# Layer 2: the normalisation of a pair's rows moves from VectorE to ScalarE, ahead of the second gate

## The chip, the cores and the metric

One core of a Trainium2 chip runs the whole program. The metric is device time in microseconds (us). Five engines work beside each other, each through its own queue in program order: PE (TensorE), DVE (VectorE), ACT (ScalarE), POOL (GpSimd) and SP, which only starts transfers here. They meet through semaphores.

## What is computed

Two layers over x of 2 x 1024 tokens by 256. Each layer normalises the tokens, runs an attention and a feed-forward block on them, and adds attention times silu(feed-forward) to x. The change is in layer 2, whose attention runs between the two batch rows of a token (so it is small), and whose feed-forward is two linear layers, each with a layer norm ahead of it:

```python
x = x + s * g                       # end of layer 1
xn = _layernorm(x, axis=-1)
s = _L1_attn_ref(xn, L1_attn_weight_qkv, L1_attn_weight_proj)
g = _silu(_L1_ffn_ref(xn, L1_ffn_w_fc, L1_ffn_w_proj))
x = x + s * g
# in _L1_ffn_ref: bitlinear(x, w) = layer_norm(x) @ ternarized(w).T (with a fine quantisation)
h = bitlinear(x, w_fc)
h = jax.nn.gelu(h, approximate=False)
return bitlinear(h, w_proj)
```

## The kernel before, in words

The 2048 tokens are 16 tiles of 128 (one token to a partition, 256 values in a row). Layer 1 (attention with 16 query heads, and 64 experts with gathered tokens) fills the first 300 us. Layer 2 takes the tiles in eight pairs: pair p holds tiles p and p + 8, which are the two rows of the batch for the same 128 positions.

The order of layer 2 is written out by hand, once for each engine, as a loop over p from -3 (`AHEAD` = 3) to 7. Turn p of every loop works on several pairs at once: it ends pair p, runs the hidden layer of pair p + 1, takes the moments of pair p + 2, and gates layer 1's output of pair p + 3. There is no scheduler; a queue does what its loop says, in that order.

- VectorE, turn p: `low_x(p+1)` (L1213, the low half of the turned x), `sum_squares(p)` (L1250), `moments(p+2)` (L1182 to L1191: statistics of the pair's rows, the last two steps each 128 x 2 numbers from `mv1` into `nv`), `spreads(p)` (L1256 to L1259: the variance for pair p's second norm, with L1258 squaring 128 x 2 numbers of `st3`), `low(p+1,0)` (L1243), `newton(p)` (L1150 to L1152, after GpSimd's root), `half_scale(p)` (L1267, `zhalf`), `normalise(p+2)` (L1203: rows minus mean, times 1/std, into `xh`; then two small steps for `kvscale`), `products(p+1)`, `low(p+1,1)`, `score_difference(p+1)`, `silu2(p)` (L1275), `silu(p+3)` (L1172), `low(p+1,2)`, `attended(p)` (L1284) and `low(p+1,3)`. Each `low` needs ScalarE's `square` of the same quarter.
- ScalarE, turn p: `high_x(p+1)`, `half_tanh(p)`, two quarters of the hidden layer (`hidden(p+1,0)`, `hidden(p+1,1)`, each gelu L770, copy L777, square L783), `take_attT(p)`, `gate(p+3)`, `take_kv(p+1)` (L762, L763), `gate2(p)` (L808, which waits for `zhalf`), then quarters 2 and 3.
- GpSimd, turn p: `weigh(p)` (L524), `total(p+3)` (L505, L506), `gated(p+3)` (L512), `roots(p)` (L537: the power -0.5 of all variances), `add_gated(p+3)` (L517, after VectorE's `silu`), `finish(p)` (L531, after VectorE's `attended`). Turn 5 and later have no `total` and no `gated`, since there is no pair p + 3.
- TensorE, turn p: `turn_x(p+1)` (transposes of `xh`), `down1(p, 0..3)` (L1647, after `silu2(p-1)`; quarter 3 needs `low(p,3)`), `fc(p+1, 0..1)`, `turn_att(p)`, `square_sums(p)` (L1654), `qkv(p+1)`, `fc(p+1, 2..3)`, `project(p)`.

TensorE's part of a turn comes about half a turn behind VectorE's. A "loop" below is the time from one start of `roots` (L537) to the next.

Of the kernel before, what the change touches and what calls it, by code (L numbers as in the profile page):

```python
# [9 lines left out]
ACT = mybir.ActivationFunctionType  # L10
ALU = mybir.AluOpType
AX = mybir.AxisListType

P = 128
# [50 lines left out]
NP = NT // 2  # L65
GT = 2
# [22 lines left out]
def build(nc, q, router, Wkv, Wo, shared, sd, wgu_d, wdn_d, wqkv, wpo, wpo4, wfc, wpj, out):  # L89
# [9 lines left out]
    with ExitStack() as ctx:  # L99
        def sb(name, shape, dt=F32):  # L100
            return ctx.enter_context(nc.sbuf_tensor(name, shape, dt))

        def sem(name):
            return ctx.enter_context(nc.semaphore(name))
# [3 lines left out]
        def bk_(i):  # L108
            return two[i // 2][:, (i % 2) * 512:(i % 2) * 512 + 512]


        x = sb("x", [P, NT, D])
# [98 lines left out]
        def l1(n):  # L211
            at[0] += n
            assert at[0] <= 10752, at
            return F[:, at[0] - n:at[0]]

        xh = [l1(GT * D).rearrange("p (q d) -> p q d", q=GT) for _ in range(2)]
# [32 lines left out]
        mv1 = sb("mv1", [P, GT, 2])  # L249
        st3 = sb("st3", [P, 2, GT])  # L250
        msq, ratio = sb("msq", [P, GT]), sb("ratio", [P, GT])
        kvscale, zhalf = [[sb(f"{n}{i}", [P, GT]) for i in range(2)] for n in ("kvscale", "zhalf")]
        gwc = sb("gwc", [P, 1])
        nv, ny, nt2 = [sb(n, [P, 3 * GT]) for n in ("nv", "ny", "nt2")]
        expo = sb("expo", [P, 3 * GT])
        warm = sb("warm", [P, 1])
# [36 lines left out]
        acc_ready, gated_ready, gate_ready, silu_ready, x1_ready, xh_ready, xT1_ps, xT_hi_ready, xT_lo_ready = [  # L293
            sem(n) for n in ("acc_ready", "gated_ready", "gate_ready", "silu_ready", "x1_ready", "xh_ready", "xT1_ps",
                             "xT_hi_ready", "xT_lo_ready")]
# [3 lines left out]
        cs_ps, wpj2_ready, wpo_ready, fc_ps, gelu_ready, sq_ready, sqsum_ready, zhalf_ready, hi_ready, lo_ready = [  # L299
            sem(n) for n in ("cs_ps", "wpj2_ready", "wpo_ready", "fc_ps", "gelu_ready", "sq_ready", "sqsum_ready",  # L300
                             "zhalf_ready", "hi_ready", "lo_ready")]
        v_in, root_ready = sem("v_in"), sem("root_ready")
        z_ps, ztanh_ready, zu_ready, out_ready, out_last, out_stored = [sem(n) for n in (
            "z_ps", "ztanh_ready", "zu_ready", "out_ready", "out_last", "out_stored")]

# [34 lines left out]
        def root_cols(p):  # L340

            return slice(0 if p + 2 < NP else 2 * GT, 3 * GT if p >= 0 else 2 * GT)
# [69 lines left out]
        def _(pool):  # L412
# [120 lines left out]
            def roots(p):  # L533

                c = root_cols(p)
                pool.wait_ge(v_in, p + 3)
                pool.tensor_tensor(ny[:, c], nv[:, c], expo[:, c], ALU.pow).then_inc(root_ready, 1)  # L537

            for p in range(-AHEAD, NP):
                if p >= 0:  # L540
                    weigh(p)
                if 0 < p + AHEAD < NP:
                    total(p + AHEAD)
                    gated(p + AHEAD)
                if p >= -2:
                    roots(p)
                if 0 < p + AHEAD < NP:
                    add_gated(p + AHEAD)
                if 0 <= p < LAST:
                    finish(p)  # L550

        @block.scalar
        def _(sc):
# [181 lines left out]
            def gate(p):  # L735
                if p:
                    sc.wait_ge(acc_ready, p)
                else:
                    sc.wait_ge(tot_first, 1)
                if p == 2:  # L740
                    sc.wait_ge(x1_first, 1)
                elif p > 2:
                    sc.wait_ge(x1_ready, p - 2)
                for q_ in range(GT):
                    t = p + NP * q_
                    sc.activation(tg[p % 2][:, q_, :], tot[:, t, :], ACT.Tanh, scale=half_rden[:, t:t + 1]).then_inc(gate_ready, 1)

            def high_x(p):
                sc.wait_ge(xT1_ps, p + 1)
                if p:  # L750
                    sc.wait_ge(fc_ps, FC * p)
                    sc.wait_ge(qkv_ps, p)
                sc.activation(xT_hi, bk_(0).rearrange("p (k n) -> p k n", k=KH), ACT.Copy).then_inc(xT_hi_ready, 1)

            def take_kv(p):

                sc.wait_ge(scale_ready, p + 1)
                sc.wait_ge(qkv_ps, p + 1)
                if p >= 2:
                    sc.wait_ge(attT_ps, p - 1)  # L760
                old = bk_(1)[:, QKV1:512].rearrange("p (g c) -> p g c", g=NKV1)
                sc.activation(kv0[p % 2], old, ACT.Copy, scale=kvscale[p % 2][:, 0:1])  # L762
                sc.activation(own[p % 2][:, 0], old[:, :, HD1:2 * HD1], ACT.Copy, scale=kvscale[p % 2][:, 0:1])\  # L763
                    .then_inc(kv_ready1, 1)
# [21 lines left out]
            def hidden(p, j):  # L786

                if p < NP:
                    gelu(p, j)
                    high(p, j)  # L790
                    square(p, j)

            def half_tanh(p):
                sc.wait_ge(dif_ready, p + 1)
                if p:
                    sc.wait_ge(tdv_ready, p)
                sc.activation(td[:, :], dif[:, :], ACT.Tanh, scale=kvscale[p % 2][:, 1:2]).then_inc(td_ready, 1)

            def take_attT(p):
                sc.wait_ge(attT_ps, p + 1)  # L800
                sc.activation(attT, bk_(6)[:, 0:3 * P].rearrange("p (k n) -> p k n", k=3), ACT.Copy).then_inc(attT_ready, 1)

            def gate2(p):
                sc.wait_ge(zhalf_ready, p + 1)
                if p:
                    sc.wait_ge(zu_ready, GT * p)
                for q_ in range(GT):
                    sc.activation(tz[:, q_, :], z_bank(q_)[:, 0:D], ACT.Tanh, scale=zhalf[p % 2][:, q_:q_ + 1])\  # L808
                        .then_inc(ztanh_ready, 1)

            for p in range(-AHEAD, NP):
                if 0 <= p + 1 < NP:
                    high_x(p + 1)
                if p >= 0:
                    half_tanh(p)
                if p + 1 >= 0:
                    hidden(p + 1, 0)
                    hidden(p + 1, 1)
                if p >= 0:
                    take_attT(p)  # L820
                if p + AHEAD < NP:
                    gate(p + AHEAD)
                if 0 <= p + 1 < NP:
                    take_kv(p + 1)
                if p >= 0:
                    gate2(p)
                if p + 1 >= 0:
                    hidden(p + 1, 2)
                    hidden(p + 1, 3)

        @block.vector
        def _(ve):
# [7 lines left out]
            def then(ins):  # L840
                ve.wait_ge(dve, mark(ins))
# [261 lines left out]
            for n in range(NE):  # L1103
                ve.wait_ge(gtanh_ready, n + 1)
                if n >= 2:
                    ve.wait_ge(hT_ps, n - 1)
                then(ve.scalar_tensor_tensor(out=h[n % 2], in0=eth[n % 2], scalar=1.0, in1=gu[n % 2][:, 0:FF],  # L1107
                                             op0=ALU.add, op1=ALU.mult))
# [89 lines left out]
            def normalise(p):  # L1198

                if p >= 2:  # L1200
                    ve.wait_ge(xT1_ps, p - 1)
                for q_ in range(GT):
                    ve.tensor_scalar(xh[p % 2][:, q_, :], x[:, p + NP * q_, :], mv1[:, q_, 0:1], ny[:, GT + q_:GT + q_ + 1],  # L1203
                                     ALU.subtract, ALU.mult).then_inc(xh_ready, 1)
                then(ve.tensor_tensor(ratio[:, :], nv[:, GT:2 * GT], ny[:, GT:2 * GT], ALU.mult))
                if p >= 2:
                    ve.wait_ge(kv_ready1, p - 1)
                ve.scalar_tensor_tensor(out=kvscale[p % 2][:, :], in0=ny[:, 0:GT], scalar=1.0 / WSCALE, in1=ratio[:, :],
                                        op0=ALU.mult, op1=ALU.mult).then_inc(scale_ready, 1)
# [88 lines left out]
            for p in range(-AHEAD, NP):  # L1298
# [14 lines left out]
                if 0 <= p + 2 < NP:  # L1313
                    normalise(p + 2)
# [413 lines left out]
```

## Time and profile before

| what | value |
|---|---|
| time, median of 3 runs (lowest, highest) | 428.29 us (426.84, 429.66) |
| the profiled execution's own time | 431.49 us |
| its span, first to last instruction | 429.8 us |
| busy: PE, PEld | 342.5 us (80%), 268.9 us (63%) |
| busy: DVE | 301.1 us (70%) |
| busy: ACT | 209.4 us (49%) |
| busy: POOL | 252.3 us (59%) |

The shares are means over the whole span; layer 2 is its last quarter, and each engine's share there is another. Busy is what an engine spent in instructions, and an instruction that is held up inside counts as busy for all of that time. In a timeline the start of an instruction may lie a tenth before the end of the one ahead of it on its engine, because they overlap; the step from start to start is then what one of them costs its engine.

### The profile page before, as it was taken

What the parts mean: (1) busy time and instruction counts of PE and PEld (TensorE: products, weight loads), DVE (VectorE), ACT (ScalarE), POOL (GpSimd) and SP (SyncE); (2) the same over time, 40 slices, a digit from 0 to 9 for tenths busy, and PEclk for the clock granted to TensorE, in tenths of its full rate; (3) what the DMA queues carried; (4) which work ended last, traced back from release to release, by engine and by line L of the source; (5) the groups of instructions that cost most, each with busy time, mean ns of one, the idle gap of its engine ahead of it and who ended that gap; (6) DMA issues with size and microseconds to landing.
All of it is one profiled execution on the core that took longest, in us unless ns stands there. A gap on an engine that the chain in (4) does not pass through costs nothing.

```text
span 429.8 us, 7084 instructions
## 1 busy us (share of the span) xinstructions
PE 342.5 (80%) x2108; PEld 268.9 (63%) x2108; DVE 301.1 (70%) x950; ACT 209.4 (49%) x536; POOL 252.3 (59%) x237
## 2 busy tenths in 40 slices
PE   0997688997989898989889888694078878987893
PEld 0983345675767677767676676483056766776773
DVE  4699744647858765546575656844668998899875
ACT  3734235444623463564343344321147678676871
POOL 3682034756867766678887888754456545764211
PEclk9999599998989999999999999979569999999999
DMA  8855933557775879878778786534920000000001
GB/s 281 350 179 152 361 97 95 108 119 174 158 184 115 230 173 278 247 174 198 144 177 187 148 193 138 90 38 56 317 69 0 26 2 25 26 25 27 2 24 51
DMA packets 33033, 58.42 MB, mean 136 GB/s; under 512 B 3723, under 2 KB 20451, under 8 KB 32611
## 3 DMA queue, kind: packets, MB, share of 16 engines
q1 hardware_dynamic: 20707, 39.08, 27.8%
q0 software_dynamic: 12288, 18.88, 24.6%
q8 instruction: 18, 0.29, 0.3%
q14 instruction: 20, 0.16, 0.1%
HBM read 40.22 MB, written 17.73 MB: 135 GB/s over the span
## 4 chain that ended last, share of the span: by engine, by line
PE 35%; DVE 26%; issue 11%; DMA 10%; ACT 9%; POOL 6%; DVEq 0%; POOLq 0%; SPq 0%; ACTq 0%
PE two L1523 5%; PE two L1503 5%; DMA W<-tok_d,idxE 4%; DMA acc_d<-W,idxE 4%; PE two L1463 4%; PE two L1535 4%; DVE F L1250 3%; PE two L1388 2%; POOL ny L537 2%; PE two L1512 2%; ACT W L783 2%; POOL W L478 2%; ACT two L770 2%; POOL acc_d L497 2%; PE two L1414 2%
## 5 line engine op out<-in xcount | busy, mean ns | idle before, releaser
L497 POOL DMA_INDIRECT acc_d<-W,idxE x64 | 103.3, 1614 | 48.9 <-DVE W L1071 30.6
L478 POOL DMA_INDIRECT W<-tok_d,idxE x56 | 57.4, 1025 | 41.6 <-DVE idxE L1033 24.8
L1107 DVE SCALAR_TENSOR_TENSOR W<-W,two 128x88 f32<-128x88 f32 x64 | 15.5, 242 | 57.8 <-ACT W L702 45.1
L686 ACT ACTIVATE W<-two 128x256 f32<-128x256 f32 x64 | 24.4, 380 | 43.6 <-PE two L1512 39.0
L1503 PE MATMUL two<-A,v 128*128 128x128 f32 x256 | 34.9, 295 | 6.7 <-issue 5.9
L1503 PEld LDWEIGHTS two<-A,v 128*128 128x128 f32 x256 | 33.7, 208 | 9.5 <-issue 8.9
L1647 PE MATMUL two<-W,A 128*128 128x257 f16 x256 | 30.1, 273 | 11.3 <-DVE F L1275 10.0
L1614 PE MATMUL two<-F,wfcT 128*128 128x256 f16 x256 | 32.8, 280 | 4.3 <-DVE A L1243 2.9
L1647 PEld LDWEIGHTS two<-W,A 128*128 128x128 f16 x256 | 23.9, 98 | 17.2 <-DVE F L1275 11.8
L770 ACT ACTIVATE two<-two,gwv 128x512 f32<-128x512 f32 x32 | 21.3, 665 | 23.3 <-PE two L1614 23.3
L1463 PE MATMUL two<-kT,vT 128*128 128x512 f32 x64 | 30.4, 597 | 2.6 <-DVE F L1024 1.4
L1523 PE MATMUL two<-W 128*128 128x176 f32 x160 | 31.9, 324 | 0.0
L1512 PE MATMUL two<-ident,W 128*128 128x128 f32 x112 | 22.7, 286 | 11.0 <-DMA W<-tok_d,idxE 9.9
L1071 DVE TENSOR_SCALAR W<-two,W 128x256 f32<-128x256 f32 x56 | 26.8, 478 | 5.8 <-PE two L1535 2.8
L1614 PEld LDWEIGHTS two<-F,wfcT 128*128 128x128 f16 x256 | 24.9, 100 | 9.4 <-issue 4.2
L1512 PEld LDWEIGHTS two<-ident,W 128*128 128x128 f32 x112 | 14.5, 146 | 24.1 <-DMA W<-tok_d,idxE 14.2
L952 DVE TENSOR_REDUCE nmax<-two 128x1 f32<-128x1024 f32 x16 | 19.6, 1223 | 11.8 <-PE two L1463 9.9
L517 POOL TENSOR_TENSOR x<-x,F 128x512 f32<-128x512 f32 x7 | 8.9, 1272 | 31.3 <-DVE F L1172 31.3
L1523 PEld LDWEIGHTS two<-W 128*128 128x128 f32 x160 | 25.1, 198 | 0.6 <-issue 0.4
L1535 PE MATMUL two<-W 88*128 88x256 f32 x80 | 24.3, 385 | 1.1 <-DVE W L1071 0.7
L1243 DVE TENSOR_TENSOR A<-two,A 128x512 f16<-128x512 f32 x32 | 21.9, 683 | 2.5 <-ACT W L783 2.0
L663 ACT ACTIVATE A<-two,nmax 128x1024 f32<-128x1024 f32 x16 | 17.8, 1114 | 11.7 <-DVE nmax L952 10.3
(239 smaller groups left out, 877.6 us busy)
## 6 DMA issues: line engine op xcount, KB each, us to landing
W<-in_gu SPq DMA_DIRECT2D x20, 352.0 KB
acc_d<-F SPq DMA_DIRECT2D x2, 2176.0 KB, 14.5
F<-in_gu SPq DMA_DIRECT2D x12, 352.0 KB
W<-in_dn SPq DMA_DIRECT2D x20, 176.0 KB
tok_d<-xr SPq DMA_DIRECT2D x2, 1280.0 KB, 5.8
F<-in_dn SPq DMA_DIRECT2D x12, 176.0 KB
x<-in_q SPq DMA_DIRECT2D x4, 512.0 KB, 6.6
A<-in_Wo SPq DMA_DIRECT2D x1, 2048.0 KB, 12.9
```

Of the source, the lines that this page charges most:

```text
L478: pool.indirect_dma_start(out=xg[n % XR], out_offset=None, in_=tok_d[:, :], in_offset=bass.IndirectOffsetOnAxis(ap=idxE[:, n:n + 1], axis=0))\
L497: pool.indirect_dma_start(out=acc_d[n % 2][:, :], out_offset=bass.IndirectOffsetOnAxis(ap=idxE[:, n:n + 1], axis=0), in_=ysb[n % YS], in_o ...
L686: sc.activation(xgT[n % 2], bk_(2)[:, 0:D].rearrange("p (k n) -> p k n", k=KH), ACT.Copy)\
L770: sc.activation(fc_bank(n), fc_bank(n), ACT.Gelu, scale=gwv[:, 0:1]).then_inc(gelu_ready, 1)
L1071: ve.tensor_scalar(ysb[n % YS], bk_(3)[:, 0:D], xg[n % XR][:, D + n:D + n + 1], 0.5, ALU.mult, ALU.mult)\
L1463: ins = pe.matmul(two[2][:, 512 * h:512 * h + 512], vT[:, rows], kT[:, at:at + 512], start=True, stop=True)
L1503: ins = pe.matmul(bk_(1)[:, 0:P], v[:, (ORDER[t] // NP) * NP + i, :], probT[t % 2][:, i, :], start=(i == 0), stop=(i == 7))
L1512: ins = pe.transpose(bk_(2)[:, P * k:P * k + P], xg[n % XR][:, P * k:P * k + P], ident[:, :])
L1523: ins = pe.matmul(gu[n % 2], xgT[n % 2][:, k, :], wgu[r][:, n % WG, k, :], start=(k == 0), stop=(k == KH - 1))
L1535: pe.matmul(bk_(3)[:, 0:D], hT[n % 2], wdn[(n // WG) % WR][:, n % WG, :], start=True, stop=True)\
L1614: ins = pe.matmul(to, wfcT[:, k, P * c:P * c + P], part[:, k, :], start=(i == 0), stop=(i == 3))
L1647: pe.matmul(z_bank(q_)[:, 0:D + 1], part[p % 2][:, at:at + P], wpj2[:, c, 0:D + 1], start=(c == 0 and part is hiT), stop=(c == FF1 // P - ...
```

## The change

For pairs 1 to 7 VectorE no longer writes the normalised rows. It forms `shift` = -mean x 1/std (128 x 2 numbers) and gives a semaphore; ScalarE then makes each row tile as Identity(scale x row + shift), two instructions of 128 x 256, between `take_kv(p+1)` and `gate2(p)`. Pair 0 stays on VectorE. GpSimd's `roots` now waits until the rows of the pair before have been written, since ScalarE reads the same `ny`.

```diff
--- before.py
+++ after.py
@@ -251,6 +251,7 @@
         msq, ratio = sb("msq", [P, GT]), sb("ratio", [P, GT])
         kvscale, zhalf = [[sb(f"{n}{i}", [P, GT]) for i in range(2)] for n in ("kvscale", "zhalf")]
         gwc = sb("gwc", [P, 1])
+        shift = [sb(f"shift{i}", [P, GT]) for i in range(2)]
         nv, ny, nt2 = [sb(n, [P, 3 * GT]) for n in ("nv", "ny", "nt2")]
         expo = sb("expo", [P, 3 * GT])
         warm = sb("warm", [P, 1])
@@ -299,7 +300,7 @@
         cs_ps, wpj2_ready, wpo_ready, fc_ps, gelu_ready, sq_ready, sqsum_ready, zhalf_ready, hi_ready, lo_ready = [
             sem(n) for n in ("cs_ps", "wpj2_ready", "wpo_ready", "fc_ps", "gelu_ready", "sq_ready", "sqsum_ready",
                              "zhalf_ready", "hi_ready", "lo_ready")]
-        v_in, root_ready = sem("v_in"), sem("root_ready")
+        v_in, root_ready, shift_ready = sem("v_in"), sem("root_ready"), sem("shift_ready")
         z_ps, ztanh_ready, zu_ready, out_ready, out_last, out_stored = [sem(n) for n in (
             "z_ps", "ztanh_ready", "zu_ready", "out_ready", "out_last", "out_stored")]
 
@@ -534,6 +535,8 @@
 
                 c = root_cols(p)
                 pool.wait_ge(v_in, p + 3)
+                if p >= -1:
+                    pool.wait_ge(xh_ready, GT * min(p + 2, NP))
                 pool.tensor_tensor(ny[:, c], nv[:, c], expo[:, c], ALU.pow).then_inc(root_ready, 1)
 
             for p in range(-AHEAD, NP):
@@ -752,6 +755,15 @@
                     sc.wait_ge(qkv_ps, p)
                 sc.activation(xT_hi, bk_(0).rearrange("p (k n) -> p k n", k=KH), ACT.Copy).then_inc(xT_hi_ready, 1)
 
+            def normalise(p):
+
+                sc.wait_ge(shift_ready, p)
+                if p >= 2:
+                    sc.wait_ge(xT1_ps, p - 1)
+                for q_ in range(GT):
+                    sc.activation(xh[p % 2][:, q_, :], x[:, p + NP * q_, :], ACT.Identity, bias=shift[p % 2][:, q_:q_ + 1],
+                                  scale=ny[:, GT + q_:GT + q_ + 1]).then_inc(xh_ready, 1)
+
             def take_kv(p):
 
                 sc.wait_ge(scale_ready, p + 1)
@@ -822,6 +834,8 @@
                     gate(p + AHEAD)
                 if 0 <= p + 1 < NP:
                     take_kv(p + 1)
+                if 0 < p + 2 < NP:
+                    normalise(p + 2)
                 if p >= 0:
                     gate2(p)
                 if p + 1 >= 0:
@@ -1199,9 +1213,13 @@
 
                 if p >= 2:
                     ve.wait_ge(xT1_ps, p - 1)
-                for q_ in range(GT):
-                    ve.tensor_scalar(xh[p % 2][:, q_, :], x[:, p + NP * q_, :], mv1[:, q_, 0:1], ny[:, GT + q_:GT + q_ + 1],
-                                     ALU.subtract, ALU.mult).then_inc(xh_ready, 1)
+                if p:
+                    ve.scalar_tensor_tensor(out=shift[p % 2][:, :], in0=mv1[:, :, 0], scalar=-1.0, in1=ny[:, GT:2 * GT],
+                                            op0=ALU.mult, op1=ALU.mult).then_inc(shift_ready, 1)
+                else:
+                    for q_ in range(GT):
+                        ve.tensor_scalar(xh[0][:, q_, :], x[:, NP * q_, :], mv1[:, q_, 0:1], ny[:, GT + q_:GT + q_ + 1],
+                                         ALU.subtract, ALU.mult).then_inc(xh_ready, 1)
                 then(ve.tensor_tensor(ratio[:, :], nv[:, GT:2 * GT], ny[:, GT:2 * GT], ALU.mult))
                 if p >= 2:
                     ve.wait_ge(kv_ready1, p - 1)
```

On ScalarE's queue, around the second gate of a steady turn. `two` is PSUM, `F` holds the work tiles of layer 2, and `F<-x,shift,ny` is the new step. Before:

```order
L762 ACTIVATE F<-two,kvscale 128x128
L763 ACTIVATE F<-two,kvscale 128x64
L808 ACTIVATE F<-two,zhalf 128x256 x2
L770 ACTIVATE two<-two,gwv 128x512
L777 ACTIVATE A<-two 128x512
L783 ACTIVATE W<-two 128x2x256
L770 ACTIVATE two<-two,gwv 128x512
L777 ACTIVATE A<-two 128x512
L783 ACTIVATE W<-two 128x2x256
```

After:

```order
L774 ACTIVATE F<-two,kvscale 128x128
L775 ACTIVATE F<-two,kvscale 128x64
L764 ACTIVATE F<-x,shift,ny 128x256 x2
L820 ACTIVATE F<-two,zhalf 128x256 x2
L782 ACTIVATE two<-two,gwv 128x512
L789 ACTIVATE A<-two 128x512
L795 ACTIVATE W<-two 128x2x256
L782 ACTIVATE two<-two,gwv 128x512
L789 ACTIVATE A<-two 128x512
L795 ACTIVATE W<-two 128x2x256
```

Two instructions now stand ahead of `gate2` (L808 before, L820 after) and of all that follows it.

On VectorE's queue, in the same turn, from `half_scale` (L1267 before, L1285 after) on. Before:

```order
L1267 TENSOR_SCALAR zhalf<-ny,gwc 128x2
L1203 TENSOR_SCALAR F<-x,mv,ny 128x256 x2
L1205 TENSOR_TENSOR ratio<-nv,ny 128x2
L1208 SCALAR_TENSOR_TENSOR kvscale<-ny,ratio 128x2
L1223 SCALAR_TENSOR_TENSOR F<-two,kvscale,F 128x128
L1225 SCALAR_TENSOR_TENSOR F<-two,kvscale,F 128x64
L1228 TENSOR_TENSOR F<-two,F 128x256
```

After:

```order
L1285 TENSOR_SCALAR zhalf<-ny,gwc 128x2
L1217 SCALAR_TENSOR_TENSOR shift<-mv,ny 128x2
L1223 TENSOR_TENSOR ratio<-nv,ny 128x2
L1226 SCALAR_TENSOR_TENSOR kvscale<-ny,ratio 128x2
L1241 SCALAR_TENSOR_TENSOR F<-two,kvscale,F 128x128
L1243 SCALAR_TENSOR_TENSOR F<-two,kvscale,F 128x64
L1246 TENSOR_TENSOR F<-two,F 128x256
```

The two wide instructions are gone and one on 128 x 2 numbers stands in their place; the rest follows in the same order.

## Rows read from the trace of the kernel before

**Rows 1.** Stretches between starts of L537: length, then PE, PEld, DVE, ACT, POOL busy.

```profile
331.98:345.65 13.67, 11.61 (x98) 9.60 (x95) 12.57 (x34) 9.98 (x23) 8.22 (x7) 1.00 0.06 20
...
373.02:386.71 13.69, 11.55 (x97) 9.59 (x95) 12.59 (x34) 9.93 (x22) 8.25 (x7) 1.00 0.06 20
386.71:399.80 13.09, 10.77 (x90) 9.01 (x89) 11.93 (x34) 9.14 (x20) 4.45 (x4) 1.00 0.07 22
```

**Rows 2.** Timeline, VectorE, one turn: start us, us, engine, line, op, out<-in.

```profile
371.17 0.17 DVE L1189 TENSOR_SCALAR nv<-mv 128x2 f32<-128x2 f32 x1
371.37 0.17 DVE L1191 TENSOR_SCALAR nv<-mv 128x2 f32<-128x2 f32 x1
...
371.83 0.91 DVE L1258 TENSOR_TENSOR msq<-st 128x2 f32<-128x2 f32 x1
...
374.99 0.23 DVE L1267 TENSOR_SCALAR zhalf<-ny,gwc 128x2 f32<-128x2 f32 x1
375.12 0.73 DVE L1203 TENSOR_SCALAR F<-x,mv,ny 128x256 f32<-128x256 f32 x2
375.77 0.15 DVE L1205 TENSOR_TENSOR ratio<-nv,ny 128x2 f32<-128x2 f32 x1
...
379.02 0.68 DVE L1243 TENSOR_TENSOR A<-two,A 128x512 f16<-128x512 f32 x1
...
380.40 0.68 DVE L1243 TENSOR_TENSOR A<-two,A 128x512 f16<-128x512 f32 x1
```

**Rows 3.** Timeline, GpSimd, the end of one turn and the next.

```profile
371.45 1.27 POOL L512 TENSOR_TENSOR A<-A,W 128x512 f32<-128x512 f32 x1
...
380.56 1.27 POOL L531 TENSOR_TENSOR x<-x,F 128x512 f32<-128x512 f32 x1
...
385.15 1.27 POOL L512 TENSOR_TENSOR A<-A,W 128x512 f32<-128x512 f32 x1
```

**Rows 4.** Timeline, ScalarE, from the second gate on, same turn.

```profile
375.25 0.84 ACT L808 ACTIVATE F<-two,zhalf 128x256 f32<-128x256 f32 x2 [0.61 <-DVE zhalf L1267]
...
377.16 0.62 ACT L783 ACTIVATE W<-two 128x512 f32<-128x512 f32 x1
...
378.85 0.64 ACT L783 ACTIVATE W<-two 128x512 f32<-128x512 f32 x1
```

**Rows 5.** Source line L569, ScalarE: duration ns min/median/max of its 12 instructions.

```profile
L569 ACT ACTIVATE xr<-x,nmr,rstd x12: 585/591/607, 9.3 to 21.3; 128x256 f32<-128x256 f32 x12
```

**Rows 6.** Timeline, ScalarE, the pair of L569 at the start of the kernel.

```profile
9.26 1.08 ACT L569 ACTIVATE xr<-x,nmr,rstd 128x256 f32<-128x256 f32 x2
```

**Rows 7.** Timeline, ScalarE, turn -1, the square of quarter 3.

```profile
325.03 0.63 ACT L783 ACTIVATE W<-two 128x512 f32<-128x512 f32 x1
```

**Rows 8.** Timeline, VectorE, the first turns and one late one.

```profile
309.15 1.25 DVE L1191 TENSOR_SCALAR nv<-mv 128x2 f32<-128x2 f32 x1
...
316.52 1.24 DVE L1189 TENSOR_SCALAR nv<-mv 128x2 f32<-128x2 f32 x1
...
320.75 0.74 DVE L1203 TENSOR_SCALAR F<-x,mv,ny 128x256 f32<-128x256 f32 x2
...
325.76 0.69 DVE L1243 TENSOR_TENSOR A<-two,A 128x512 f16<-128x512 f32 x1 [0.47 <-ACT W L783]
...
330.22 0.83 DVE L1189 TENSOR_SCALAR nv<-mv 128x2 f32<-128x2 f32 x1
...
411.49 0.23 DVE L1256 TENSOR_SCALAR st<-two 128x2 f32<-128x2 f32 x2 [1.43 <-PE two L1654]
```

**Rows 9.** Timeline, GpSimd, the first turns.

```profile
309.11 1.27 POOL L512 TENSOR_TENSOR A<-A,W 128x512 f32<-128x512 f32 x1
...
316.47 1.26 POOL L506 TENSOR_TENSOR W<-W,xr 128x512 f32<-128x512 f32 x1
...
329.75 1.27 POOL L512 TENSOR_TENSOR A<-A,W 128x512 f32<-128x512 f32 x1
331.98 1.33 POOL L537 TENSOR_TENSOR ny<-nv,expo 128x6 f32<-128x6 f32 x1 [0.96 <-DVE nv L1259]
```


## The prediction

> **What bounds the kernel now.** I read the busy time by stretches first, then the timelines of VectorE, ScalarE and GpSimd over one turn, and then asked for each wait in the turn which of its sources comes last. A loop (L537 to L537) takes 13.67 to 13.69 us in four turns running, and 13.09 in the one after [rows 1]. In it VectorE shows 12.59 us busy, ScalarE 9.93, TensorE 11.55. So VectorE looks like the bound, and work taken off it looks like gain. But its busy time holds a stall: L1258, 128 x 2 numbers, took 0.91 us, while the small steps L1189 and L1191 beside it took 0.17 [rows 2]. It ended at 372.74, and GpSimd's L512 ended at 372.72 (371.45 + 1.27) [rows 3]. L1189 at 330.22 was stretched to 0.83 and ended at 331.05, where GpSimd's L512 ended at 331.02 [rows 8, 9]. A small VectorE step between SBUF tiles that begins while a GpSimd instruction runs thus ends with it. The four equal loops are closed by this: from the start of `half_scale` (L1267, 374.99) to quarter 2's L1243 at 379.02 is 4.03 us; GpSimd's L531, which waits for the `attended` behind it, starts 1.54 later (380.56); its row L512 ends at 386.42, 5.86 later [rows 2, 3]; L1258 ends there, L537 starts 0.29 behind (386.71 [rows 1]), and 1.97 us after that the next `zhalf` is written (373.02 to 374.99; the same distance holds each turn). 4.03 + 1.54 + 5.86 + 0.29 + 1.97 = 13.69: the whole loop.
>
> ScalarE's half runs beside the first term. Its gate starts at 375.25 and its squares of quarters 2 and 3 end at 377.78 (377.16 + 0.62) and 379.49 [rows 4]; VectorE takes them at 379.02 and 380.40 [rows 2]. So they lie 1.24 and 0.91 us ahead of need. That is all the slack there is for new work ahead of the gate.
>
> **The change part by part.**
>
> VectorE loses the two L1203: from 375.12 to L1205 at 375.77 is 0.65 us a pair, and gains one step on 128 x 2 numbers. Such a step costs its queue 0.09 to 0.20 us (0.16 long, partly overlapped); I take 0.10. That is 0.55 us a pair, seven pairs, 3.8 us of busy time.
>
> ScalarE gains two 128 x 256 instructions with scale and bias read per partition. The same form is in the trace: L569, median 591 ns [rows 5], the pair 1.08 us from first start to last end, so 0.49 from start to start and 0.98 for the pair [rows 6]. A cheap bound is L808 itself (scale alone, source in PSUM): the pair 0.84 us [rows 4], about 0.78 from start to start. A dear bound is 2 x 0.59 = 1.18, without overlap. I take 0.98, since the form is the same. `shift` is ready about 0.06 after `zhalf` was (0.13 behind its start, 0.16 long, against 0.23). So the gate and all behind it start D = 0.98 + 0.06 = 1.04 us later (0.84 to 1.24). The Trainium skill, "ScalarE: Activation LUTs", Rules for kernel authors, speaks against this move: adds and multiplies belong on VectorE. By its figures in What ACT_TABLE_LOAD costs such an instruction is, as an estimate, 186 + 2 x 93 + 0.833 x 256 = 585 ns, 93 of which overlap; the trace's 591 and 0.49 agree, so its pair would be 0.98 too.
>
> *Turn -1 (pair 1).* ScalarE works without a gap through `take_kv` and quarters 2 and 3, up to the square that ends at 325.66 [rows 7], and VectorE's L1243 waits for that until 325.76 [rows 8]. `shift` is ready long before (L1203 ran at 320.75 [rows 8]). So the 0.98 is paid in full: VectorE comes to L1189 at 331.2 in place of 330.22. GpSimd's L524 waits for ScalarE's `half_tanh`, which also slips 0.98, so L512 (329.75 [rows 9]) slips the same and holds L1189 again. Term A: +0.97.
>
> *Loops 1 to 4 (pairs 2 to 5).* Quarter 2's L1243 may start when the square has ended: 374.99 + 0.29 (`shift` written) + 0.03 (to ScalarE) + 0.98 + 2.53 (gate to end of that square, 375.25 to 377.78) + 0.10 (ScalarE to VectorE, 325.66 to 325.76) = 378.92. VectorE itself would be there at 379.02 - 0.55 = 378.47 and waits. So `attended`, L531 and L512 come 0.10 earlier, not 0.55. Quarter 3 comes 1.71 behind quarter 2 (the squares' distance, 377.78 to 379.49) where it came 1.38 behind: at 380.63, 0.23 later than now. From there `low_x`, `sum_squares`, `moments` run through, so L1189 slips 0.23 while L512 comes 0.10 earlier. What matters is their distance: L1189 started 0.28 before L512 (371.17, 371.45) and L1191 0.08 before (371.37) [rows 2, 3], so both got through and only L1258 was held. After the change they stand at +0.05 and +0.25. Two rows show what that does: L1191 0.04 behind an L512 (309.15, 309.11) took 1.25 us, and L1189 0.05 behind an L506 (316.52, 316.47) took 1.24 [rows 8, 9]. So L1189 is held, with L1191, L1256, L1258 and L1259 still behind it, and L537 starts as in turn -1: 0.96 after L512's end (331.02 to 331.98 [rows 9]) in place of 0.29. A loop becomes 13.69 - 0.10 + 0.67 = 14.26, +0.57; four of them, term B: +2.3. The distance hangs on 1.71 against 1.38 and not on the cost of the two new instructions, as both quarters wait for ScalarE.
>
> The Trainium skill, "SBUF — State Buffer", Who interferes with whom, has this as a lock on a port pair that VectorE and GpSimd share, held for a whole instruction: whoever issues first gets it, the other fully blocks. The trace agrees in the four stretched rows above.
>
> *Loop 5 (pair 6; 13.09 now).* No L512 stands in it; VectorE runs through, and pays between 0 and the 0.23 of quarter 3. Term C: +0.1.
>
> *Turn 5 (pair 7).* Quarter 3 comes some 0.7 later, since there is no `silu` to fill VectorE. But L1256 waits 1.43 us for TensorE there [rows 8], whose `down1` starts 0.5 earlier and needs quarter 3 last. Both about cancel: 0. Turns 6 and 7 normalise nothing: 0.
>
> TensorE's transposes of `xh` have the rows at about 376.4, when TensorE comes free for them; GpSimd's new wait in `roots` is for rows written a turn earlier. Both cost 0, and 0.1 a pair if ScalarE is at the dear bound.
>
> Sum: 0.97 + 2.3 + 0.1 = 3.4 us on a span of 429.8, or on the execution's own 431.49, which is 3.2 above the median of the runs. On the median, 428.29 + 3.4 = **431.7**.
>
> **The rivals.**
>
> *Quarter by quarter it just balances (L1189 and L1191 get through).* If ScalarE's distance between quarters is made up somewhere (0.1 us would do for L1189, 0.3 for both), L512 catches L1191 alone, L537 then 0.75 after L512 (0.96 less the 0.20 from L1189 to L1191 [rows 2]): 4 x (0.46 - 0.10) + 1.07 = +2.5, 430.8; or neither, and the loops gain 0.10 each: 0.97 - 0.4 + 0.1 = +0.7, 429.0. For it: the 0.05 is thin. Against: two rows at the same distance.
>
> *Slower by more than 1%: ScalarE becomes the loop.* At the dear bound, 0.20 more in every turn: quarter 2 then comes 0.10 later than now, and the loop is 14.46; 1.17 + 4 x 0.77 + 0.3 + 0.1 = +4.7, 433.0. It decides from 0.17 us more a pair than my 0.98. Against it: L569's rows, 12 of them between 585 and 607 ns.
>
> *Faster: VectorE's busy time is the bound after all.* 0.55 x 7 = -3.8, 424.4. It needs ScalarE to have 1.04 us to spare ahead of quarter 3, and it has 0.91, and none in turn -1.
>
> **How the numbers follow.** Forecast (L1189 held) 50%; L1191 alone 17%; neither held 11%; ScalarE slower 17%; faster 5%. The range runs from 428.6, just under the case of +0.7, to 433.6, just over the dear bound, and leaves out the fast case and the tails of a measurement that spread from 426.84 to 429.66. Within 1% (4.3 us, about what a measurement can tell from no change) lie the first three cases nearly whole; slower by more are the dear case and the upper tail of the forecast, whose 3.4 is 0.9 below the bound: 0.22. Faster by more than 1%: 0.02. Same: 0.76.
>
> **What would show it.** In the timeline after: the new pair on ScalarE starting about 0.03 behind `shift`, 0.98 until the gate; quarter 2's and 3's `low` each waiting for ScalarE's square; L1203 (today's L1189) about 1.3 us long in four turns and L1276 (today's L1258) 0.16 in all; loops of 14.3 us where 13.7 stood; and turn -1 about 1 us longer. VectorE's busy time hardly falls, for its stall is longer. Wrong would be: L1203 at 0.17 (term B falls), a loop under 13.6 (ScalarE had slack), or TensorE waiting for `xh`.

## The result, and the profile after

The changed kernel is slower by about one per cent: 433.75 us median against 428.73 for the kernel before in the same comparison, a ratio of 1.0109 with a 95% interval of 1.0058 to 1.016. On 428.29 us that is +4.7 us (2.5 to 6.9); the prediction was +3.4, 431.7. The profiled execution spans 432.6 us against 429.8.

The change acts in layer 2. These are the steps from one start of `roots` (L537 before, L540 after) to the next, beginning with the second; the first is turn -1, the next five are loops 1 to 5 of the prediction:

| loop | before | after | difference | predicted |
|---|---|---|---|---|
| turn -1 | 12.88 | 13.87 | +0.99 | +0.97 |
| 1 | 13.67 | 14.27 | +0.60 | +0.57 |
| 2 | 13.69 | 14.26 | +0.57 | +0.57 |
| 3 | 13.68 | 14.25 | +0.57 | +0.57 |
| 4 | 13.69 | 14.27 | +0.58 | +0.57 |
| 5 | 13.09 | 13.17 | +0.08 | +0.1 |
| turn 5 | 12.38 | 12.62 | +0.24 | 0 |
| turn 6 | 10.59 | 10.60 | +0.01 | 0 |
| sum | 103.67 | 107.31 | +3.64 | +3.4 |

The profiled span grew by only 2.8 because the first start of `roots` came 0.80 us earlier after (309.68) than before (310.48). Nothing ahead of it was changed; over all profiled executions of this study that start lies between 305.14 and 310.48. A time over the whole kernel therefore carries the scatter of layer 1, and the loops are the finer measure. They come from one profile of each kernel; that the four middle loops of a profile agree within 0.02 us in both kernels shows how steady they are.

Loops 4 and 5 of the changed kernel by busy time, the lines that answer to [rows 1] (length, then PE, PEld, DVE, ACT and POOL busy with their instructions):

```profile
374.94:389.21 14.27, 11.78 (x95) 9.44 (x95) 12.55 (x33) 10.91 (x25) 8.23 (x8) 1.00 0.06 19
389.21:402.38 13.17, 10.84 (x88) 8.92 (x89) 11.51 (x33) 9.77 (x21) 4.44 (x5) 1.00 0.07 22
```

VectorE is busy 12.55 us of 14.27, where it was busy 12.59 of 13.69, though 0.57 us of work has left it in each loop. ScalarE went from 9.93 to 10.91. The timeline of ScalarE shows where its new work stands, ahead of the gate (L820, L808 before) and its squares (L795, L783 before), as in [rows 4]:

```profile
377.24 1.09 ACT L764 ACTIVATE F<-x,shift,ny 128x256 f32<-128x256 f32 x2 [1.02 <-DVE shift L1217]
378.23 0.81 ACT L820 ACTIVATE F<-two,zhalf 128x256 f32<-128x256 f32 x2
...
380.13 0.63 ACT L795 ACTIVATE W<-two 128x512 f32<-128x512 f32 x1
...
381.82 0.63 ACT L795 ACTIVATE W<-two 128x512 f32<-128x512 f32 x1
```

The pair of L764 takes 0.99 from its start to the gate, and starts 0.04 behind the end of `shift`. ScalarE had waited 1.02 us for it, so it had time, but in a place where it could not be used. On VectorE the same turn reads (start, us, line; compare [rows 2]):

```profile
376.91 0.23 DVE L1285 TENSOR_SCALAR zhalf<-ny,gwc 128x2 f32<-128x2 f32 x1
377.05 0.15 DVE L1217 SCALAR_TENSOR_TENSOR shift<-mv,ny 128x2 f32<-128x2 f32 x1
...
379.77 0.68 DVE L1186 SCALAR_TENSOR_TENSOR F<-F,A 128x512 f32<-128x512 f32 x1
380.85 0.69 DVE L1261 TENSOR_TENSOR A<-two,A 128x512 f16<-128x512 f32 x1 [0.39 <-issue]
381.45 0.87 DVE L1302 SCALAR_TENSOR_TENSOR F<-two,zhalf,F 128x256 f32<-128x256 f32 x2
382.54 0.69 DVE L1261 TENSOR_TENSOR A<-two,A 128x512 f16<-128x512 f32 x1 [0.22 <-issue]
...
387.00 1.27 DVE L1203 TENSOR_SCALAR nv<-mv 128x2 f32<-128x2 f32 x1
388.31 0.17 DVE L1205 TENSOR_SCALAR nv<-mv 128x2 f32<-128x2 f32 x1
...
388.77 0.16 DVE L1276 TENSOR_TENSOR msq<-st 128x2 f32<-128x2 f32 x1
```

and GpSimd, as in [rows 3]:

```profile
382.40 1.27 POOL L532 TENSOR_TENSOR x<-x,F 128x512 f32<-128x512 f32 x1 [0.60 <-DVE F L1302]
...
386.98 1.27 POOL L513 TENSOR_TENSOR A<-A,W 128x512 f32<-128x512 f32 x1
389.21 1.33 POOL L540 TENSOR_TENSOR ny<-nv,expo 128x6 f32<-128x6 f32 x1 [0.96 <-DVE nv L1277]
```

The idle time ahead of the two quarters carries no releaser in these rows ("issue"). In loop 1 the same two steps have it, ScalarE's square (L795), and here they start 0.09 us behind the ends of the squares (380.76 and 382.45):

```profile
338.07 0.69 DVE L1261 TENSOR_TENSOR A<-two,A 128x512 f16<-128x512 f32 x1 [0.40 <-ACT W L795]
339.77 0.69 DVE L1261 TENSOR_TENSOR A<-two,A 128x512 f16<-128x512 f32 x1 [0.23 <-ACT W L795]
```

Quarter 2 (L1261 at 380.85) starts 3.94 us behind `zhalf` (4.03 before) and quarter 3 (382.54) 5.63 (5.41 before). The first small step of `moments`, L1203, starts at 387.00, 0.02 behind GpSimd's gated product (386.98), lasts 1.27 in place of 0.17, and ends at 388.27, where that product ends (388.25). L1276, the step that took 0.91 us before, takes 0.16. `roots` starts 0.96 behind the product's end in place of 0.29.

### The profile page after: what moved, and what is told of

Read it like the earlier page. It is cut to its first block, busy times and chain, and to the rows that moved or that the text cites. A ratio compares the mean times of both kernels' runs of the same rounds, so it can differ in the third digit from the quotient of the medians.

```text
span 432.6 us, 7106 instructions
## 1 busy us (share of the span) xinstructions
PE 344.8 (80%) x2108; PEld 269.1 (62%) x2108; DVE 300.4 (69%) x943; ACT 216.0 (50%) x550; POOL 253.3 (59%) x237
## 4 chain that ended last, share of the span: by engine, by line
PE 40%; DVE 26%; issue 11%; ACT 10%; DMA 8%; POOL 4%; POOLq 0%; DVEq 0%; SPq 0%; ACTq 0%
PE two L1541 6%; PE two L1521 6%; PE two L1481 5%; PE two L1553 5%; DMA W<-tok_d,idxE 4%; DVE F L1268 3%; PE two L1530 3%; PE two L1406 2%; PE two L1492 2%; POOL ny L540 2%; DMA acc_d<-W,idxE 2%; ACT two L782 2%; PE two L1432 2%; ACT W L795 2%; DVE nv L1203 1%
## 5 line engine op out<-in xcount | busy, mean ns | idle before, releaser
L1541 PE MATMUL two<-W 128*128 128x176 f32 x160 | 33.1, 333 | 0.0
L1261 DVE TENSOR_TENSOR A<-two,A 128x512 f16<-128x512 f32 x32 | 22.1, 689 | 7.6 <-ACT W L795 3.5
L1541 PEld LDWEIGHTS two<-W 128*128 128x128 f32 x160 | 26.1, 205 | 0.6 <-issue 0.4
```

What stands on the lines that cost most here:

```text
L1541: ins = pe.matmul(gu[n % 2], xgT[n % 2][:, k, :], wgu[r][:, n % WG, k, :], start=(k == 0), stop=(k == KH - 1))
```

## Experiments

Two theories were put against each other. **L** (the held step): both quarters now wait for ScalarE, 1.7 us apart in place of 1.4; so VectorE's small steps come later and GpSimd's gated product earlier, the product now catches the first of them and not the fourth (L1189, L1191, L1256, L1258 in the kernel before), and all behind it is late. **W** (the waits): a loop grows as VectorE waits for ScalarE's squares, and where the held time stands costs nothing new. Times below over the whole kernel are ratios against the kernel before, with the 95% interval; "the sum" is that of the table above (103.67 before, 107.31 changed). Loops and sums are from one profile of each version.

### ScalarE's delay alone, VectorE unchanged

On the kernel before:

```diff
+        spare = kT[:, 0:GT * D].rearrange("p (q d) -> p q d", q=GT)
...
+            def beside_gate(p):
+
+                if p >= 2:
+                    sc.wait_ge(zhalf_ready, p - 1)
+                for q_ in range(GT):
+                    sc.activation(spare[:, q_, :], x[:, p + NP * q_, :], ACT.Identity, bias=gwv[:, 0:1], scale=gwv[:, 1:2])
...
                     take_kv(p + 1)
+                if 0 < p + 2 < NP:
+                    beside_gate(p + 2)
```

> The kernel before, its normalisation left whole on VectorE, with two extra ScalarE instructions of the same form and size (Identity, 128 x 256, scale and bias read per partition) into an unused tile, ahead of the second gate in turns -1 to 5. So only ScalarE's delay is added. Theory L (the held small step): turn -1 about 0.98 us longer; in loops 1 to 4 quarter 2 is still taken when VectorE comes to it (square ended 378.76, need 379.02), quarter 3 comes 0.17 later; L1189 stands 0.11 before GpSimd's L512 and gets through, the step after it (0.09 behind L512's start) is held about 1.2 us, L537 starts 0.75 after L512's end, a loop is 14.15. Theory W (the loop grows only by VectorE's waits for ScalarE's squares, the held step costs nothing new): 13.69 + 0.17 = 13.86. On the time: L +3.0 us against before, W +1.9.

Measured: ratio 1.0074 (1.0027 to 1.012), +3.2 us; loops 1 to 4 are 14.13, 14.13, 14.15 and 14.14, turn -1 is 13.86, the sum 106.65, 2.98 above before (L +3.0, W +1.9). One turn on VectorE and GpSimd:

```profile
356.89 0.17 DVE L1199 TENSOR_SCALAR nv<-mv 128x2 f32<-128x2 f32 x1
357.10 1.21 DVE L1201 TENSOR_SCALAR nv<-mv 128x2 f32<-128x2 f32 x1
...
358.60 0.16 DVE L1268 TENSOR_TENSOR msq<-st 128x2 f32<-128x2 f32 x1
```

```profile
357.01 1.27 POOL L513 TENSOR_TENSOR A<-A,W 128x512 f32<-128x512 f32 x1
```

The first small step starts 0.12 ahead of the product (expected 0.11) and takes 0.17. The second starts 0.09 behind it and takes 1.21. Quarter 3 was only 0.15 to 0.17 us late here, and the loop grew by 0.45. W, which allows 0.17, falls. Neither what VectorE was spared nor the new waits on `shift` and in `roots` are needed for a loss of nearly the changed kernel's size; that its loops are 0.12 longer still goes with the first step being held there and only the second here (`roots` 0.96 behind the product's end against 0.75 to 0.76), less the 0.09 by which quarter 2 comes earlier there.

### One row tile on each engine

```diff
-                for q_ in range(GT):
+                for q_ in (1,):
                     sc.activation(xh[p % 2][:, q_, :], x[:, p + NP * q_, :], ACT.Identity, bias=shift[p % 2][:, q_:q_ + 1],
...
                                             op0=ALU.mult, op1=ALU.mult).then_inc(shift_ready, 1)
+                    ve.tensor_scalar(xh[p % 2][:, 0, :], x[:, p, :], mv1[:, 0, 0:1], ny[:, GT:GT + 1],
+                                     ALU.subtract, ALU.mult).then_inc(xh_ready, 1)
```

> One of the two row tiles on each engine: ScalarE makes tile 1 of a pair, VectorE tile 0, right behind the new small step. Theory L: ScalarE is delayed 0.55 in place of 1.04, VectorE relieved 0.23; both quarters are taken when VectorE comes to them, both 0.23 earlier, so the distance between the first small step of moments and GpSimd's gated product stays at -0.28, only the square of the means is held, and a loop is 13.46, shorter than before; turn -1 is 0.49 longer; the total against before is -0.6 us. Theory W (half of ScalarE's load, half of the loss): a loop of 13.98, +1.8 us.

Measured: ratio 1.0008 (0.9969 to 1.0047); loops 13.43, 13.44, 13.41 and 13.43 (13.46 expected, 13.98 by W), turn -1 13.39, the sum 102.68, 1.0 below before (0.6 expected). The times over the whole kernel don't show that gain: the interval runs from 0.3% faster to 0.5% slower. The order of the steps is that of the kernel before, with the square of the means held again:

```profile
354.33 0.18 DVE L1203 TENSOR_SCALAR nv<-mv 128x2 f32<-128x2 f32 x1
354.54 0.17 DVE L1205 TENSOR_SCALAR nv<-mv 128x2 f32<-128x2 f32 x1
...
355.00 0.90 DVE L1278 TENSOR_TENSOR msq<-st 128x2 f32<-128x2 f32 x1
```

```profile
354.62 1.27 POOL L513 TENSOR_TENSOR A<-A,W 128x512 f32<-128x512 f32 x1
```

Half the work moved gains 0.25 us a loop, and all of it costs 0.58. The effect of the move is no straight line in its size. ScalarE's delay was about 0.55 us with half of it and 1.04 with all of it; by the prediction's count the slack ahead of quarter 3 was 0.91. So half fits into it, and with all of it the phase against GpSimd flips. Where between the two it flips was not measured.

### GpSimd's product out of the way

On the changed kernel, and on the kernel before:

```diff
-            def total(p):
+            def both_halves(p):
                 pool.wait_ge(acc_ld[p], 32)
                 then(pool.tensor_tensor(pair(tot, p), pair(tot, p), pair(acc1, p), ALU.add))
+
+            def total(p):
+                if p <= AHEAD:
+                    both_halves(p)
...
                     roots(p)
+                if p >= 0 and p + AHEAD + 1 < NP:
+                    pool.wait_ge(scale_ready, p + 3)
+                    both_halves(p + AHEAD + 1)
```

> The changed kernel, with GpSimd's first addition of the total of pair p + 4 (pairs 4 to 7) taken out of the busy end of the turn into its idle stretch before the add of the gated product, once kvscale of pair p + 2 is written. GpSimd's chain from the end of pair p to the gated product is then 4.5 us in place of 5.86. Theory L: the gated product ends before the first small step of moments, nothing is held, a loop is 10.09 (zhalf to that step, as measured) + 1.11 + 1.97 = 13.17 in place of 14.26, and the time falls 4.3 us against the changed kernel, to about 0.7 below before. Theory W: the loop stays at 14.2 or falls at most by the 0.3 that VectorE's last waits leave, and the time stays 4 us above before.

> The kernel before with the same move of GpSimd's first addition. Theory L: the gated product ends 10.08 us behind zhalf, where L1189 stands at 9.86, so L1189 is held about 0.2; L537 0.96 behind, 1.97 more to the next zhalf: a loop of 13.0 in place of 13.69, and -2.8 us in all against before. With the first addition moved in both kernels the change costs only quarter 3's 0.2 a loop and turn -1's 0.98: this kernel is 1.8 us faster than the changed kernel with the same move. Theory W: 13.69 stays (VectorE never waited there).

Measured on the changed kernel: ratio 0.996 (0.992 to 1.0001); loops 13.17, 13.16, 13.21 and 13.15 where 14.26 stood; the sum 102.94, 4.37 less than the changed kernel's. On the kernel before: ratio 0.9948 (0.9906 to 0.999); loops 13.01, 13.01, 13.01 and 13.00, the sum 101.39, 2.28 below before (2.8 expected; its turn -1 is 13.27, see below). The two intervals overlap, so that the second is the faster one stands in the sums alone (1.55 us; 1.8 expected). A turn of the first:

```profile
355.11 0.17 DVE L1210 TENSOR_SCALAR nv<-mv 128x2 f32<-128x2 f32 x1
355.31 0.17 DVE L1212 TENSOR_SCALAR nv<-mv 128x2 f32<-128x2 f32 x1
...
355.77 0.16 DVE L1283 TENSOR_TENSOR msq<-st 128x2 f32<-128x2 f32 x1
```

```profile
345.65 1.27 POOL L506 TENSOR_TENSOR W<-W,F 128x512 f32<-128x512 f32 x1 [1.27 <-DVE kvscale L1233]
...
350.50 1.26 POOL L536 TENSOR_TENSOR x<-x,F 128x512 f32<-128x512 f32 x1 [0.53 <-DVE F L1309]
...
353.72 1.27 POOL L517 TENSOR_TENSOR A<-A,W 128x512 f32<-128x512 f32 x1
356.21 1.33 POOL L544 TENSOR_TENSOR ny<-nv,expo 128x6 f32<-128x6 f32 x1 [1.21 <-DVE nv L1284]
```

The product (L517) ends at 354.99, before the first small step at 355.11; nothing is held. ScalarE's load and both waits for its squares are as in the changed kernel, and yet 1.1 us a loop are gone. In one of its four loops, the one of 13.21, the product came later and held that step for 0.05 us (0.22 in place of 0.17). In the kernel before with the same edit a hold of 0.06 is left in every loop (0.23 in place of 0.17; 0.2 was expected). So with the hold all but gone the move costs 13.17 - 13.01 = 0.16 us a loop, which is about the 0.21 that quarter 3 is late by (5.63 behind `zhalf` against 5.42), less the 0.06.

### Pair 1 left on VectorE too

```diff
-                sc.wait_ge(shift_ready, p)
+                sc.wait_ge(shift_ready, p - 1)
...
-                if 0 < p + 2 < NP:
+                if 1 < p + 2 < NP:
                     normalise(p + 2)
...
-                if p:
+                if p > 1:
                     ve.scalar_tensor_tensor(out=shift[p % 2][:, :], ...
```

> The changed kernel with pair 1 left on VectorE too, so that turn -1 is that of the kernel before. Theory L: the loop of turn -1, which ScalarE fills, goes back from 13.87 to 12.9 us; loops 1 to 4 stay at 14.26, loop 5 at 13.17 and turn 5 at 12.6; in all 1.0 us less than the changed kernel. Rival (the loss of turn -1 is a start-up effect that the next loops would show instead): the first or second loop grows by about 1 us.

Measured: ratio 1.0029 (0.9999 to 1.006); loops 1 to 4 are 14.26, 14.26, 14.25 and 14.25, loop 5 13.16, turn 5 12.62: no later loop pays. But turn -1 is 13.35, not 12.9, so 0.52 less than the changed kernel's, and the sum is 106.74, 0.57 less and not 1.0. What differs from the kernel before in that turn is TensorE's clock. The granted clock (third number from the right) in the last us ahead of turn -1 and in its first three (two for the kernel before):

```profile
318.10:319.10 1.00, 1.00 (x9) 0.74 (x7) 0.00 (x0) 0.97 (x3) 1.00 (x1) 0.82 0.00 0
319.10:320.10 1.00, 1.00 (x12) 0.74 (x11) 0.63 (x1) 0.97 (x3) 1.00 (x2) 1.00 0.00 0
320.10:321.10 1.00, 1.00 (x12) 0.90 (x10) 0.90 (x6) 1.00 (x3) 0.03 (x1) 1.00 0.00 0
```

```profile
316.82:317.82 1.00, 1.00 (x7) 0.73 (x5) 0.00 (x0) 0.97 (x3) 1.00 (x1) 0.50 0.00 0
317.82:318.82 1.00, 1.00 (x5) 0.48 (x4) 0.65 (x1) 0.97 (x3) 1.00 (x2) 0.50 0.00 0
318.82:319.82 1.00, 1.00 (x6) 0.51 (x4) 0.88 (x6) 1.00 (x3) 0.02 (x1) 0.50 0.00 0
319.82:320.82 1.00, 1.00 (x13) 0.94 (x11) 0.61 (x4) 1.00 (x4) 0.00 (x0) 0.80 0.00 0
```

In the kernel before it was at 2.4 GHz when turn -1 began; here it stayed at half of that, 1.2 GHz, for two us of the turn, and rose in the third. The matmuls for quarter 2 end later, and ScalarE waits for them:

```profile
320.77 0.31 ACT L775 ACTIVATE F<-two,kvscale 128x64 f32<-128x64 f32 x1
321.32 0.66 ACT L782 ACTIVATE two<-two,gwv 128x512 f32<-128x512 f32 x1 [0.24 <-PE two L1632]
```

The kernel before with GpSimd's early addition shows the same (turn -1 13.27, the clock at 0.50 in both of those us, the same wait of 0.24), although nothing ahead of turn 0 was edited in it. In the version with ScalarE's delay alone the clock rose late too and turn -1 is still 13.86: ScalarE's extra work hides the lateness of the matmuls. So the 0.99 of turn -1 holds against an early rise of the clock, and against a late one the move costs 0.5 to 0.6 there (13.86 less 13.35 or 13.27). Only the profiles of the kernel before and of the changed kernel have the early rise; in the other eight the clock is at 0.50 through the first us of turn -1. A sum that is compared with 103.67 carries up to 0.4 us of that. Why the clock rose when it did, these runs don't show.

### Behind quarter 2

```diff
-                if 0 < p + 2 < NP:
-                    normalise(p + 2)
                 if p >= 0:
                     gate2(p)
                 if p + 1 >= 0:
                     hidden(p + 1, 2)
+                    if 0 < p + 2 < NP:
+                        normalise(p + 2)
                     hidden(p + 1, 3)
```

> The changed kernel with ScalarE's two new instructions moved behind quarter 2 of the hidden layer, ahead of quarter 3, so behind the second gate. ScalarE's load is the same. Theory L: quarter 2 is then taken when VectorE comes to it, 3.46 behind zhalf in place of 3.94, so GpSimd's gated product ends 10.87 behind zhalf; quarter 3 stays at 5.6, the first small step of moments at 10.09 and is held until that end; L537 0.96 behind: a loop of 10.87 + 0.96 + 1.97 = 13.80, against 14.26 changed and 13.69 before. Theory W (the loop follows ScalarE's last square): 14.26 stays. In all L: 1.9 us less than the changed kernel.

Measured: ratio 1.0033 (0.9995 to 1.007); loops 13.78, 13.77, 13.76 and 13.78 (13.80 expected, 14.26 by W). ScalarE's last square ends 5.45 behind `zhalf`, within 0.1 of the changed kernel's 5.54, but `attended`, and with it GpSimd's chain, goes half a us earlier; the first small step is still held, for a shorter time. The total was missed: the sum is 106.00, 1.3 below the changed kernel and not 1.9, since turn 5 grew to 13.11 and turn -1 to 14.05. In turn -1 the clock was late (0.50 in its first us, 0.54 in its second), and quarter 2, no longer behind ScalarE's extra work, is late with it. In turn 5 TensorE's transposes of `xh` wait for ScalarE, and `down1` stands behind them:

```profile
405.93 0.66 PE L1606 MATMUL two<-ident,F 128*128 128x128 f32 x4 [1.78 <-ACT F L764]
406.42 3.68 PE L1665 MATMUL two<-W,A 128*128 128x257 f16 x32
```

### Two versions that beat both

The early addition, now for pairs 3 to 7, was put together with pairs 0 and 1 on VectorE and one row tile on each engine from pair 2 on; and, as its counterpart, on the kernel before.

> Three moves together: pairs 0 and 1 on VectorE; from pair 2 on one row tile on each engine; GpSimd's first addition of the total done early for pairs 3 to 7. Theory L: turn -1 loses the held small step, 12.9 - 0.7 = 12.2; in the loops GpSimd's gated product ends 9.86 behind zhalf (3.80 + 1.55 + 4.51), the first small step of moments stands at 9.63 and is held until then, a loop is 9.86 + 0.96 + 1.97 = 12.79; loop 5 12.85, turn 5 12.13 as in the half version; from the second start of L537 to the last 98.9 us against 103.67 before: -4.8 us, 1.1% faster than before. Theory W gives no gain from GpSimd's move, so -1.0.

> The kernel before (normalisation whole on VectorE) with GpSimd's first addition early for pairs 3 to 7. Theory L: turn -1 12.2 us where TensorE's clock is up as in the kernel before, loops 13.0, loop 5 13.1, turn 5 12.4: 100.3 us from the second start of L537 to the last, -3.3 against before, 1.5 more than the version with one row tile on each engine. Theory W: no gain.

Measured: the split version 0.9932 (0.9904 to 0.9959), its loops 12.75, 12.76, 12.76 and 12.76, turn -1 12.34, the sum 98.94 (98.9 expected); the other 0.9913 (0.9872 to 0.9954), its loops 13.01, 12.99, 13.00 and 13.01, turn -1 12.70, the sum 100.79 (100.3 expected, with 12.2 in turn -1 under the early clock). Both have the late clock. W, which gives GpSimd's move no gain, falls here too. Both beat the kernel before by 0.7 to 0.9 per cent. By their loops the split version is 1.85 us ahead; the times over the whole kernel don't tell them apart.

## Why the prediction was right, point by point

- *What closes the loop.* Right: GpSimd's product and the small step held by it, not VectorE's 92% of busy time. With the product moved away the kernel before fell from 13.69 to 13.01 a loop, though VectorE's work is the same and it is still busy 11.91 us of that.
- *ScalarE's price.* 0.98 was taken for the pair; from its start to the gate it measured 0.99. `shift` was ready 0.06 behind `zhalf`, as said, and VectorE's saving 0.57 (quarter 2 would have been reached 3.46 behind `zhalf`) for 0.55.
- *Turn -1, +0.97.* Measured +0.99, with the clock as early as before. That the size hangs on the clock was not seen: against a late rise it is 0.5 to 0.6.
- *Loops 1 to 4, +0.57 each.* Measured +0.60, +0.57, +0.57 and +0.58, by the steps named: quarter 2 0.09 earlier (0.10), quarter 3 0.22 later (0.23), the first small step 0.02 to 0.04 behind the product (0.05), and held. The rival in which it gets through by a hair did not happen in any of the four turns; it did in the version with ScalarE's delay alone, 0.10 to 0.13 ahead of the product.
- *Loop 5, +0.1.* Measured +0.08.
- *Turn 5, 0.* Measured +0.24. The step that failed is "both about cancel". TensorE's `down1` did start earlier, but quarter 3, 0.8 late, held its last part: it waited 0.66 and ended 7.50 behind `zhalf` (410.81 + 1.04 - 404.35) where it had ended 7.26 (405.34 + 3.69 - 401.77). Before:

```profile
405.34 3.69 PE L1647 MATMUL two<-W,A 128*128 128x257 f16 x32 [1.55 <-DVE F L1275]
```

after:

```profile
407.35 2.81 PE L1665 MATMUL two<-W,A 128*128 128x257 f16 x24 [0.87 <-DVE F L1293]
410.81 1.04 PE L1665 MATMUL two<-W,A 128*128 128x257 f16 x8 [0.66 <-DVE A L1261]
```

- *TensorE waiting for `xh`.* The prediction named this as a sign of being wrong, and put the transposes at no cost. They did wait in turn -1:

```profile
322.49 0.66 PE L1606 MATMUL two<-ident,F 128*128 128x128 f32 x4 [1.35 <-ACT F L764]
```

  The turn still came out at +0.99, for `down1`, behind the transposes, then waited for VectorE's quarters 2 and 3 (0.18 and 0.66), which wait for ScalarE. In loops 1 to 5 and turn 5 only the weight loads waited, about 0.3 us each, with no gap in the matmuls. So the sum stands, but the sign was set too wide: a wait of TensorE that another wait follows before the turn's end need not lengthen the turn.
- *The Trainium skill.* The rule of "ScalarE: Activation LUTs", to keep adds and multiplies on VectorE, agrees with the sign for the whole move and not for half of it, which gained 0.25 us a loop. By its price the instruction takes 585 ns as an estimate, 93 of them overlapped; the 14 of L764 measured 585 to 607, median 599, and about 0.50 from start to start. The lock of "SBUF — State Buffer", Who interferes with whom, gives the mechanism of the loss, and the traces agree: the small step that starts ahead of the product runs, the one that starts behind it ends 0.01 to 0.04 us after it.
- *The time.* The loops add to +3.64, the runs say +4.7 with an interval from 2.5 to 6.9. The rest isn't explained, and needs no cause beyond the scatter.
- *The dear rival* (433.0) lies nearer to the measured median than the forecast, but its mechanism was not there: it needed 1.18 for ScalarE's pair.

## What to carry to other kernels

Before work is taken off a busy engine, split its busy time into work and holds: an instruction on 256 numbers that lasts 0.9 us is a wait in disguise, and what ends it is the bound. When a loop is closed by two engines that exclude each other, ask of each edit how it shifts one against the other; 0.3 us of shift was worth 0.67 us of loop here, and moving 1.3 us of GpSimd's work into its idle stretch was worth more (0.68 a loop) than leaving half of the moved rows on VectorE (0.25). Idle time of an engine is worth something only where it lies: ScalarE waited 1.02 us right ahead of its new work, and behind it had 0.91 us of slack for a delay of 1.04.

## What the runs showed of the hardware

A VectorE step on 128 x 2 numbers between SBUF tiles that started 0.07 to 0.13 us ahead of a GpSimd instruction of 1.27 us took its usual 0.17; started 0.02 to 0.11 behind, it took 1.17 to 1.27 and ended 0.01 to 0.04 behind that instruction. Between 0.07 ahead and 0.02 behind no run has a start. That the border is this sharp, and that the pattern repeats in loops 1 to 4 of both kernels to some 0.02 us, was not expected. Nor was it that kernels alike up to there meet TensorE's rise from 1.2 to 2.4 GHz up to some 3 us earlier or later against their own instructions (inside the us ahead of turn -1 in the kernel before, at 0.82; in the third us of that turn where pair 1 stays on VectorE), which was worth about 0.4 us in turn -1 (12.88 against 13.27).
